# Gate columns folded into the score and value matrices of a cross-attention and expert-choice kernel

## What is computed

```python
x = x + xattn(layernorm(x), ctx, Wq, Wk, Wv, Wo, bo)      # x (2, 2048, 512), ctx (2, 77, 384), 8 heads of 64
x = x + ffn(layernorm(x), gate_w, w1, w2)

def ffn(x, gate_w, w1, w2):                                # 8 experts, 512 tokens each, hidden 2048
    scores = einsum('ntd,ed->nte', x, gate_w)
    probs = softmax(scores, axis=-1)
    g, m = top_k(probs.transpose(0, 2, 1), 512)
    h = gelu(einsum('nekd,edf->nekf', x[batch_idx, m], w1), approximate=False)
    h = einsum('nekf,efd->nekd', h, w2)
    return zeros_like(x).at[batch_idx, m].add(g[..., None] * h)
```

## Time and profile before

| | |
|---|---|
| median of 3 runs | 1743.86 us (1743.60 to 1744.99) |
| the profiled execution | 1744.05 us, of which the trace spans 1742.3 us |
| PE | busy 1708.6 us (98% of the span), 8502 matmul records |
| DVE | busy 1097.7 us (63%) |
| ACT | busy 806.0 us (46%) |
| POOL | busy 329.9 us (19%) |
| granted TensorE clock | 0.994 of full speed over the span |

### The profile page before, as it was taken

One profiled execution on the slowest core, in us unless ns is written; L12 is line 12 of the kernel. 1 busy time (PEld: TensorE's weight loads), 2 busy tenths in 40 slices (PEclk: granted clock), 3 DMA queues, 4 the chain that ended last, 5 costly groups with the idle time before them and its releaser, 6 DMA issues.

```text
span 1742.3 us, 22913 instructions
## 1 busy us (share of the span) xinstructions
PE 1708.6 (98%) x8502; PEld 1432.4 (82%) x8502; DVE 1097.7 (63%) x2012; ACT 806.0 (46%) x1786; POOL 329.9 (19%) x355
## 2 busy tenths in 40 slices
PE   7999999989999999999999999999999999999997
PEld 6799988877788888888888888888888888888886
DVE  5545577777677665765575667666765665575563
ACT  3565655463333333544454445444544544454441
POOL 2222322120113020410061007000600150032002
PEclk9999999999999999999999999999999999999999
DMA  3233235242434334331143116111521251133003
GB/s 127 73 115 127 96 128 176 84 138 93 121 121 132 135 84 158 87 107 56 66 84 111 49 49 137 58 49 59 135 73 49 67 127 49 49 74 72 25 1 49
DMA packets 76125, 156.30 MB, mean 90 GB/s; under 512 B 4436, under 2 KB 4590, under 8 KB 76023
## 3 DMA queue, kind: packets, MB, share of 16 engines
q1 hardware_dynamic: 61687, 121.38, 20.5%
q0 software_dynamic: 14336, 33.56, 9.7%
HBM read 121.37 MB, written 33.55 MB: 89 GB/s over the span
## 4 chain that ended last, share of the span: by engine, by line
PE 93%; DVE 3%; ACT 1%; issue 1%; DMA 1%; POOL 1%; SPq 0%; DVEq 0%; POOLq 0%; ACTq 0%
PE ps L1780 10%; PE ps L1781 10%; PE ps L1779 10%; PE ps L1758 9%; PE ps L1759 9%; PE ps L1757 9%; PE ps L1663 4%; PE ps L1650 3%; PE ps L1665 3%; PE ps L1664 3%; PE ps L1652 3%; PE ps L1651 3%; PE ps L958 3%; PE ps L959 3%; PE ps L960 3%
## 5 line engine op out<-in xcount | busy, mean ns | idle before, releaser
L1779 PE MATMUL ps<-v2h,hhS 128*128 128x512 f32 x768 | 300.7, 392 | 0.0
L1780 PE MATMUL ps<-v2l,hhS 128*128 128x512 f32 x768 | 298.9, 389 | 0.0
L1781 PE MATMUL ps<-v2h,hlS 128*128 128x512 f32 x768 | 298.9, 389 | 0.0
L1757 PE MATMUL ps<-Th,Wh 128*128 128x512 f32 x672 | 261.4, 389 | 0.0
L1758 PE MATMUL ps<-Tl,Wh 128*128 128x512 f32 x672 | 261.4, 389 | 0.0
L1759 PE MATMUL ps<-Th,Wl 128*128 128x512 f32 x672 | 261.4, 389 | 0.0
L1195 POOL DMA_INDIRECT out_dram<-YS,tok_idx x48 | 83.0, 1728 | 806.1 <-DVE YS L1557 797.8
L1318 ACT ACTIVATE v2h<-w_raw 128x512 fp32r<-128x512 f32 x96 | 57.8, 626 | 305.6 <-PE ps L1781 305.6
L1557 DVE SCALAR_TENSOR_TENSOR YS<-ps,tok_gate,YS 128x512 f32<-128x512 f32 x144 | 106.8, 750 | 132.1 <-PE ps L1781 132.1
L1779 PEld LDWEIGHTS ps<-v2h,hhS 128*128 128x128 f32 x768 | 144.2, 188 | 30.0 <-DVE hlS L1540 0.6
L1781 PEld LDWEIGHTS ps<-v2h,hlS 128*128 128x128 f32 x768 | 144.1, 188 | 29.8
(11 more groups left out here) (210 smaller groups left out, 3340.4 us busy)
## 6 DMA issues: line engine op xcount, KB each, us to landing
w_raw<-in_L_ffn_w_dram SPq DMA_DIRECT2D x80, 1024.0 KB, 5.1
XB<-in_x_dram SPq DMA_DIRECT2D x16, 512.0 KB, 4.0
XR<-in_x_dram SPq DMA_DIRECT2D x16, 512.0 KB, 3.4
out_dram<-X SPq DMA_DIRECT2D x16, 512.0 KB, 4.7
xn_rows<-XN SPq DMA_DIRECT2D x16, 512.0 KB, 5.4
w_raw<-in_L_xattn_Wq_dram SPq DMA_DIRECT2D x1, 1024.0 KB, 9.4
w_raw<-in_L_xattn_Wo_dram SPq DMA_DIRECT2D x1, 1024.0 KB, 12.6
w_raw<-in_L_xattn_Wk_dram SPq DMA_DIRECT2D x1, 768.0 KB, 6.4
```

What stands on the lines that cost most here:

```text
L1757: nc.tensor.matmul(ps[:, bank, :], wh, th, start=(idx in OPENS and k == 0), stop=False, **go_on)
L1779: nc.tensor.matmul(ps[:, bank, :], th, wh, start=(t == 0), stop=False)
L1780: nc.tensor.matmul(ps[:, bank, :], th, wl, start=False, stop=False)
L1781: last = nc.tensor.matmul(ps[:, bank, :], tl, wh, start=False, stop=(t == GF - 1))
```

## The change

The gate's scores are a product of the normalised x after attention with the gate's weights. Since x after attention is x plus the output of attention, and both parts come out of matmuls, the gate's 8 columns can ride on them. The change puts 4 gate columns beside each half of A (308 columns become 312) and 4 beside each half of B (the output is now made in two halves of 260 columns instead of one of 512). It takes away, for each block, the second transposes, their copy on ACT and the gate matmuls. To put the sum right, DVE adds the two parts (`glog`), and POOL carries the mean and deviation of the first norm over several steps in `ring`, and adds a term with the mean of the second norm (`gdm`, `gfix`, `glog2`). In the setup it adds the product of Wo with the gate's weights: 16 transposes of Wo, 4 of the bias, and 24 small matmuls (`pe_gate_fold`).

The order of the steps changes with it. ACT takes both exponentials before it normalises block i-2 and copies `xTh`; the transposes of x are now written to the PSUM banks of the scores of tile 0. The residual sum is made tile by tile. The scale -1/8 of the scores is folded into K, so the maximum is one instruction. The gate comes a step earlier, and so do the rounds (from step 9), the lists (steps 14 and 15) and the gather; batch 1's rounds start one slot earlier.

```diff
@@ pe_attention: the step
+                if has(i):
+                    pe.wait_ge(v_xTl, i + 1)
                 if round_at(i - 1, 2) is not None:
                     pe_round(pe, 0, round_at(i - 1, 2))
...
                 if has(i - 1):
+                    if at(i, 1):
+                        pe.wait_ge(e_lo, len(folds))
                     pe.wait_ge(g_prob, 2 * i - 1)
...
-                if has(i - 3):
-                    pe.wait_ge(a_xn2T, i - 2)
-                    pe_gate(gate_sc)
                 if round_at(i, 0) is not None:
                     pe_round(pe, 0, round_at(i, 0))
                 if at(i, 0):
                     pe.wait_ge(e_lo, NA)
+                    pe.wait_ge(d_wo, 32)
+                    for c in range(KD):
+                        for k in range(KD):
+                            d0 = k * P + k // 2 * GC
+                            last = nc.tensor.transpose(ps[:, 4 + c, k * P:(k + 1) * P], wo_sb[:, c, d0:d0 + P], ident[:])
...
-                            last = three(ps[:, 2 * t + part, 0:HALF],
+                            last = three(ps[:, 2 * t + part, 0:SC],
...
+                if at(i, 0):
...
+                    last.then_inc(p_boT, 1)
+                    pe_gate_fold(pe)
+                if has(i - 1):
+                    pe.wait_ge(v_pTl, i)
+                    out_tile(i, 0)
                 if transposed(i, has):
                     pe.wait_ge(a_xn, i + 2)
...
+                    pe.wait_ge(a_exp, 2 * i + 1)
+                    pe_xT(i + 1)
                 if at(i, 0):
...
+                    pe.wait_ge(e_wog, 1)
                     for n in range(NA, len(folds)):
                         pe_fold(pe, n)
@@ out_tile, new
+                for h in range(2):
+                    last = three(ps[:, 4 + 2 * t + h, 0:OC],
+                                 [(pTh[0:k, t, c, :], pTl[0:k, t, c, :],
+                                   fh[0:k, bass.ds(base[c] + h * OC, OC)], fl[0:k, bass.ds(base[c] + h * OC, OC)])
+                                  for c, (_, k) in enumerate(CH)])
@@ pe_gate_fold, new
+            for c in range(KD):
+                for k in range(KD):
+                    nc.tensor.matmul(ps[:, 4, c * E:(c + 1) * E], woT[:, c, k * P:(k + 1) * P], gwT[:, k, :],
+                                     start=(k == 0), stop=(k == KD - 1))
+            for k in range(KD):
+                nc.tensor.matmul(ps[:, 6, 0:E], before_f[:], gwT[:, k, :], start=(k == 0), stop=(k == KD - 1))
+            pe.wait_ge(e_boT, 1)
+            for k in range(KD):
+                last = nc.tensor.matmul(ps[0:1, 7, 0:E], boT[:, k:k + 1], gwT[:, k, :],
+                                        start=(k == 0), stop=(k == KD - 1))
@@ act_attention: the step
                 if has(i):
-                    exp(i, 0)
-                if transposed(i, has):
-                    act_xTh(act, i + 1)
+                    exp(i, 0, u)
+                    exp(i, 1, u)
                 if has(i - 2):
...
                     act_normalise(act, X1[:, u], rs2, nb2, XN2[:, u], g_nb2, a_xn2, i - 2)
-                if has(i):
-                    exp(i, 1)
+                    act_gate_exp(act, i - 2)
+                if transposed(i, has):
+                    act_xTh(act, i + 1)
...
-                if has(i - 2) and not at(i, NBLK):
-                    act_xn2T(act, i - 2)
@@ dve_attention: the end of the step
+                if has(i - 2):
+                    dve_gate_scores(dve, i - 2)
+                if has(i):
+                    reciprocal(i, 0)
+                if has(i - 1):
+                    dve_x1(dve, i - 1, 0, 1 - u, 16 * half + 16 * u,
+                           16 * half - 16 + 16 * u if not isinstance(i, int) or i >= 3 else None)
                 if transposed(i, has):
                     dve_xTl(dve, i + 1)
+                if has(i - 2):
+                    dve_gate(dve, i - 2)
                 if has(i):
-                    reciprocals(i)
+                    reciprocal(i, 1)
@@ the rounds
-        GATED = NBLK // B + 2
+        GATED = NBLK // B + 1
@@ act_experts, pe_experts
+            act.wait_ge(p_o, NBLK * TPB)
             for n in range(2):
                 weights(n)
...
-                if n in (0, 2):
-                    pe.wait_ge(a_xn2T, NBLK - 1 + n // 2)
-                    pe_gate(gate_sc7)
-                if n == 1:
-                    pe.wait_ge(a_xn2, NBLK)
-                    pe.wait_ge(v_gsub, NBLK - 1)
-                    pe_xn2T((NBLK - 1) % 2)
```

More of the change, by code:

```diff
@@ L36 @@
 NV = 5
+GC = E // 2
+SC, OC = HALF + GC, D // 2 + GC
 def xattn_expert_choice(nc, x, ctx, wq, wk, wv, wo, bo, gate_w, w1, w2, out):
@@ L76, in xattn_expert_choice @@
         ident = fixed("ident", [P, P])
+        vals = lookup("vals", [P, B, E, NT, NV, CT], BF16)
+        hot = lookup("hot", [P, NT, P], BF16)
+        inq = lookup("inq", [P, E, NT, CT], BF16)
+        run = lookup("run", [P, E, NT])
+        run2 = lookup("run2", [P, E, NT])
+        place = lookup("place", [P, E, NT])
+        q1 = lookup("q1", [P, E, NT])
+        q2 = lookup("q2", [P, E, NT])
+        quarter = lookup("quarter", [P, E, NT])
         ones_bf = lookup("ones_bf", [P, P], BF16)
@@ L317, in act_setup @@
         def act_setup(act):
+            act.wait_ge(e_ctxT, 1)
+            for b in range(B):
+                nc.scalar.activation(gate_cols(AH, b), gate_w_cols(), ACT.Copy).then_inc(e_gw, 1)
             act_normalise(act, XB[:, 0], rs1, nb1, XN, g_nb1, a_xn, 0)
@@ L331, in dve_setup @@
                                   ps[:, 0, 0:KC * B * J]).then_inc(e_ctxT, 1)
+            dve.wait_ge(e_gw, B)
+            for b in range(B):
+                nc.vector.tensor_tensor(gate_cols(AL, b), gate_w_cols(), gate_cols(AH, b).bitcast(F32),
+                                        ALU.subtract).then_inc(e_gwl, 1)
             dve.wait_ge(d_x[0], 16)
@@ L730, in act_gate_exp @@
             act.wait_ge(v_gsub, n + 1)
-            nc.scalar.activation(gexp[:], gsub[:], ACT.Exp).then_inc(a_gexp, 1)
-        def act_xn2T(act, n):
-            act.wait_ge(p_xn2T, n + 1)
-            nc.scalar.activation(xn2T[:], ps[:, 6:8, :], ACT.Copy).then_inc(a_xn2T, 1)
+            act.wait_ge(g_rs2, n + 1)
+            for t in range(TPB):
+                last = nc.scalar.activation(gexp[:, t, :], gsub[:, t, :], ACT.Exp, scale=rs2[:, t:t + 1],
+                                            accum_out=gsum[:, t:t + 1])
+            last.then_inc(a_gexp, 1)
         def act_normalise(act, src, rs, nb, dst, ready, done, n):
@@ L869, in step @@
                     dve_round(dve, 0, round_at(i, 1))
-                if has(i - 3) and not at(i, CHOICE + 1):
-                    dve_gate_scores(dve, i - 3, gate_sc)
-                if has(i - 2):
-                    dve_x1(dve, i - 2, u, 16 * half, 16 * half - 16 if not isinstance(i, int) or i >= 4 else None)
                 if at(i, CHOICE + 1):
+                    dve_places(dve, 0, 1)
+                    dve_rows(dve, 0)
                     dve_vals(0, 0, 1)
                     dve_one_hot(0)
-                    dve_found(dve, 0, BANK[0])
-                    dve_gate_scores(dve, i - 3, gate_sc)
                 if has(i):
@@ L1133, in xattn_expert_choice @@
         TURNS_1 = tuple(range(KF // 2 + 3, KF - 1))
-        HOTS = [q for q in range(VALS_AT + 1, 3 * KF + 4) if q % KF == KF - 1 or (q % 2 == 0 and q % KF > 1)]
+        HOTS = [q for q in range(VALS_AT + 1, 3 * KF + 4)
+                if q % KF == KF - 1 or (q % KF > 1 and q % 2 == int(q < 2 * KF))]
         HOT_AT = {1: 1, **{m: HOTS[m - 2] for m in range(2, len(LOOKUPS))}}
```

417 lines of the change are left out of this document (225 added, 192 removed).

## The result

| | before | with the change |
|---|---|---|
| median of four runs | 1743.73 us | 1772.11 us (1769.41 to 1773.08) |
| span of the profiled execution | 1742.3 us | 1770.9 us |
| granted TensorE clock over the span | 0.994 | 0.979 |

A forecast was written before the change was run, and what follows sets the result against it. PE was taken to bound plain steps and the experts. Steps +2.3, setup +7.6, way to the experts -4.2, experts -4.2 and clock +6.8 made +8.3: 1752 us, 0.5% slower, range 1742 to 1762.

The forecast's parts named there:

- Plain steps: Attention steps without rounds: steps 3 to 8 take 17.24 us, PE waiting 0.96 for tile 1's product, against 18.3 before.
- The chain: Plain steps: the loop from the scores through ACT, DVE and POOL to tile 1's transposes, 17.25 us against PE's 16.28.
- the wider price: Rival on the output matmuls: 260 columns cost 143 ns instead of 121, some +4.5 us more, 1757; chance 0.12.
- the uncovered loads: Rival on the output matmuls: weight loads not covered by products, 15 steps 60 us longer; chance 0.02.
- Rounds at full clock: Attention steps with rounds, before any clock loss: 20.6 us by the sum against 19.14 before; all 15 steps 278.2.
- the layout: All four queues laid out instruction by instruction with measured durations, giving each attention step's length.
- The clock, the step that failed: Round steps: PE's waits bring the granted clock down in three of five, +4.3 us.
- The rule that was set beside the sum: Trainium skill: a loop idling each turn loses the clock each turn; all five round steps fall, +7.2 us instead of 4.3.
- The clock in the setup: Setup: 6 us of small work on PE loses +1.0 us to the clock.
- The rest of the setup: Setup without clock loss: added transposes, small matmuls and waits of step 1's transposes, together +7.6 us.
- The experts, the other step that failed: Expert stage: two gates and one second transpose go and PE has no gap, -4.2 us.
- From step 16 to the experts: From step 16 to the first expert product: 21.8 us instead of 25.98, -4.2, then +1.5 for the clock.

The follow-up runs named there:

- recip: The changed kernel with DVE's reciprocals of tile 1's sums moved ahead of the low part of the transposed x and the gate's normalisation; 1753.68 us, ratio 1.0064.
- warm: The changed kernel with PE's two waits for `cnt` in steps with rounds filled by 18 and 6 matmuls that do no work; 1763.64 us, ratio 1.0117.
- fillset: The changed kernel with a 312-column matmul that does no work behind 20 of the 24 small matmuls of the gate's fold; 1767.41 us, ratio 1.0157.
- slots: The changed kernel with batch 1's rounds in the expert stage put back into the slots of the kernel before; 1767.14 us, ratio 1.0141.
- tail: The changed kernel with 20 matmuls of 512 columns that do no work in PE's wait ahead of the experts' first product; 1768.60 us, ratio 1.0146.
- spread: The changed kernel with small matmuls of the gate's fold spread behind the four groups of scores of step 0; 1770.22 us, ratio 1.0153.

## Why the prediction was wrong

- **Plain steps: right.** 17.3 to 17.6 us against 17.24, PE waiting 0.93 to 1.29 us for POOL's `PR` against 0.96. The chain was the one laid out. recip shows that the step is 16.13 without it, against 16.28 for PE's own work. The 260 columns cost 0.12 us from one start to the next, as priced, so the wider price and the uncovered loads are both out. One reason given for that price doesn't hold: at 2.4 GHz 308 columns stream in 128 ns and 512 in 213, so the two rows lie 15 and 24 ns above streaming, not both 15. The price came from the line through both and doesn't need it. Two rows of the kernel after:

```profile
374.07 0.28 PE L1056 MATMUL ps<-BH,pTh 104*128 104x260 f32 x1
374.19 0.28 PE L1057 MATMUL ps<-BL,pTh 104*128 104x260 f32 x1
```

- **Rounds at full clock: right.** For steps 9 to 15 the layout said 20.4, 20.6, 22.0, 20.6, 20.6, 18.6, 19.1; warm measured 20.4, 20.6, 22.1, 20.6, 20.6, 18.6, 19.0, and all 15 steps take 278.95 against 278.2. Of the two waits, 2.9 and 0.9 us came where 2.8 and 1.3 were forecast (step 11 had a second one of 2.3).
- **The clock, the step that failed.** "I take three of five (+4.3, the scores are in the chain)": the clock fell in each of steps 10 to 15. Against warm, steps 9 to 15 lost 0.2, 2.6, 2.3, 2.7, 1.4, 0.6 and 1.4 us, 11.4 in all. Both the count and the size were too small. The size came from the earlier trace rows, where the clock stayed at 0.51 for 3.40 us. In steps 10 to 12 it stayed at 0.50 about twice as long (229.90 to 236.60 in the first); in steps 13 to 15 it was as long as in the earlier trace rows. Step 13 has the waits of step 10, so their length doesn't decide between the two, and what does stays open. The rule that was set beside the sum (the Trainium skill, TensorE: Matmul & The Clock Gate, section HAM oscillation — how this bites in real kernels: each turn that idles pays again) was right on the count in the steps with the long waits. The trace agrees in steps 10 to 14, and step 15 fell too; but steps 3 to 8, which idle about 1 us in each turn, never fell, so the rule can't be applied to every wait. With the size of the earlier trace rows it still gave only 7.2 for five falls.
- **The clock in the setup.** One microsecond was taken for "6 us of small work"; 10.3 us at 1.2 GHz lose half of that, 5.1. fillset bears this out: 3.0 us more work and step 1 1.9 us earlier make 4.9. The rest of the setup is 7.1 us in the trace against 7.6, and that closeness is part luck: counted from the first fold it is 8.3. No run split it further.
- **The experts, the other step that failed.** "PE has no gap there, and DVE and ACT keep ahead of it in slots 0 to 3" is wrong by 7.8 us. The first round of batch 1, asked for one slot earlier, finds DVE behind one-hot lists, weight parts and hidden parts: slots puts the wait and its clock at 5.5 us. The slow first products are another 2.4 (4.74 us at 0.50), a clock loss that the sum had not put in the experts at all. In the kernel before, PE waited before its transposes of the gathered rows, not behind them, and they took the slow stretch; now they lie ahead of the wait and the products take it. A window of the kernel before, of those transposes, shows it:

```profile
354.85:360.50 5.65, 5.35 (x24) 4.98 (x25) 4.89 (x8) 4.49 (x10) 2.21 (x4) 0.50 0.50 186
360.50:366.00 5.50, 5.50 (x32) 4.84 (x33) 2.98 (x7) 5.47 (x8) 0.00 (x0) 0.99 0.00 0
```

- **From step 16 to the experts:** 24.26 against the forecast 23.3. The waits for `PR` and `pTl` came as laid out (2.8 and 2.7 us for "two waits of about 3"); no run took this stretch apart.

In sum, of the 20 us between forecast and result (28.6 less 8.3), 7.1 are the clock in the steps, 4.1 that in the setup and 7.8 the experts, and 1.3 are small terms: 0.8 in the steps, 1.0 in step 16, and 0.5 less in the setup, where the early first fold hides 1.2.

## What to carry to other kernels

Lay the queues out with measured durations, then price the clock by itself: count every long wait of PE (here 2.9 us and another 0.9 behind it; 1 us alone did nothing in six steps) and every row of small matmuls in a repeated step as a fall of its own, and give its length a range: equal waits were followed here by 3.5 us or by 7 us at half the clock. When work is cut from the bounding engine, look in the helpers' queues for short instructions behind long waits (here a reciprocal of 0.2 us behind `xTl`); moving one line took 18 us off the median. When one engine's calls are moved earlier, read for each call what its producer does just then.

## What the runs showed of the hardware

- A TensorE that works without a gap can still lose its clock: through 4.8 us of matmuls with 8 columns (40.69 to 45.50) it was busy, and then ran 10.3 us at 1.2 GHz. In fillset a matmul of 312 columns behind 20 of the 24 cost 0.15 us apiece and kept the clock at 1.00.
- After waits of 2.9 and 0.9 us the clock stayed at 1.2 GHz for 7.0 us in step 10 and for 3.5 us in step 13 of the same execution; after waits of about 1 us in steps 3 to 8 it never fell.
- The same program order did not always lose the same: steps 1 to 15 took 290.31 us in the changed kernel and 290.27 in tail, but 285.88 in slots, 284.72 in spread and 285.53 in fillset. Such a loss has a scatter of some 5 us between executions.
- A DVE instruction of 0.18 us took 0.93 to 1.03 us beside POOL's product over 128x616, ending as that product did, five times in five in the changed kernel and never in recip, where the product had ended.
